# Normalisation and transposes of the next block between the K and V matmuls, and Q matmuls between the transposes of the query blocks

## What is computed

```python
def _layernorm(x, axis=-1, eps=1e-5):
    m = jnp.mean(x, axis=axis, keepdims=True)
    v = jnp.var(x, axis=axis, keepdims=True)
    return (x - m) / jnp.sqrt(v + eps)
...
        q = jnp.einsum('bsd,de->bse', X, Wq)
        k = jnp.einsum('bsd,de->bse', X, Wk)
        v = jnp.einsum('bsd,de->bse', X, Wv)
        scores = jnp.einsum('bqe,bke->bqk', q, k)
        causal = jnp.triu(jnp.ones((S, S), dtype=bool), k=1)
        scores = jnp.where(causal, -jnp.inf, scores)
        weights = jax.nn.softmax(scores / jnp.sqrt(jnp.asarray(k.shape[-1], scores.dtype)), axis=-1)
        return jnp.einsum('bqk,bke->bqe', weights, v)
...
        gate = jnp.einsum('bsd,hd->bsh', x, wg)
        up = jnp.einsum('bsd,hd->bsh', x, wu)
        h = jax.nn.silu(gate) * up
        return jnp.einsum('bsh,dh->bsd', h, wd)
...
    xn = _layernorm(x, axis=-1)
    s = _L0_attn_ref(xn, L0_attn_Wq, L0_attn_Wk, L0_attn_Wv)
    g = _silu(_L0_ffn_ref(xn, L0_ffn_w_gate, L0_ffn_w_up, L0_ffn_w_down))
    x = x + s * g
```

## Time and profile before

| | us |
|---|---|
| runs, lowest to highest | 2223.4 to 2234.1 |
| median of the 2 runs | 2228.7 |
| profiled execution | 2218.8 |
| its span, slowest core (core 4) | 2217.2 |
| span of the fastest core | 2193.0 |
| TensorE busy in matmuls | 1679.2 (76%) |
| ScalarE busy | 551.7 (25%) |
| VectorE busy | 535.1 (24%) |
| mean granted TensorE clock of the cores | 0.90 to 0.91 |

### The profile page before, as it was taken

The page is one execution under the profiler, slowest core; times in us unless marked ns, Lnnn a source line. Parts: engine busy times, 40 slices in busy tenths (PEclk is TensorE's granted clock), DMA queues, the critical chain, the costliest instruction groups (busy, mean ns, idle before and its releaser), DMA issues.

```text
span 2217.2 us, 24390 instructions; the slowest of 8 cores (2193.0 to 2217.2 us)
## 1 busy us (share of the span) xinstructions
PE 1679.2 (76%) x8391; PEld 804.1 (36%) x8544; DVE 535.1 (24%) x1356; ACT 551.7 (25%) x842; POOL 81.2 (4%) x149
## 2 busy tenths in 40 slices
PE   0333598898998964689989999875778787878875
PEld 0222344444444432334434444322333333333332
DVE  1000124334243344011100111003342233240430
ACT  0333433334333332211101111011222222221321
POOL 0000000000000000000000000000001000000000
PEclk9955599999999986889999999987999898989998
DMA  9998324344243341243310332037776775675934
GB/s 196 193 217 184 126 95 133 112 135 133 97 146 116 118 133 38 69 113 78 76 26 1 76 77 58 0 95 253 254 256 226 244 247 209 212 263 190 301 123 164
DMA packets 165751, 320.66 MB, mean 145 GB/s; under 512 B 105088, under 2 KB 111232, under 8 KB 143104
## 3 DMA queue, kind: packets, MB, share of 16 engines
q0 software_dynamic: 29968, 151.00, 23.9%
q1 hardware_dynamic: 124144, 149.20, 22.8%
q10 hardware_dynamic: 11520, 18.88, 2.4%
HBM read 283.41 MB, written 60.82 MB: 155 GB/s over the span
## 4 chain that ended last, share of the span: by engine, by line
PE 63%; DMA 17%; ACT 6%; another core or an unknown queue 4%; issue 4%; DVE 4%; ACTq 1%; SPq 1%; DVEq 0%; POOL 0%; POOLq 0%
PE psBC L404 11%; DMA vbuf<-vv_s 8%; PE psD L572 8%; PE psA L530 8%; PE psA L430 5%; PE psD L430 5%; PE psA L647 4%; PE psD L780 4%; PE psD L540 4%; PE psBC L540 4%; PE psBC L780 4%; DMA kbuf<-kT_s 3%; ACT xns L379 3%; PE psBC L473 3%
## 5 line engine op out<-in xcount | busy, mean ns | idle before, releaser
L404 PE MATMUL psBC<-xns,wk_b 128*128 128x512 bf16 x992 | 239.1, 403 | 27.9 <-ACT xns L379 27.1
L250 PE MATMUL psA<-ident_b,wst 128*128 128x128 bf16 x576 | 70.2, 297 | 188.9 <-DMA wst<-wg 86.3
L530 PE MATMUL psA<-xnq,wgu 128*128 128x512 bf16 x752 | 173.9, 381 | 29.1 <-DMA wgu<-wuT_s 28.3
L358 DVE TENSOR_SCALAR xnr<-xkb,mvall,rstdall 128x1024 bf16<-128x1024 f32 x80 | 61.8, 810 | 539.5 <-PE psA L370 537.2
L780 PE MATMUL psBC<-vbuf,pT 128*128 128x512 bf16 x494 | 133.8, 413 | 70.1 <-DMA vbuf<-vv_s 61.6
L572 PE MATMUL psD<-wdT_b,hact 128*128 128x512 bf16 x752 | 167.5, 379 | 22.1 <-ACT g_b L581 17.7
L404 PEld LDWEIGHTS psBC<-xns,wk_b 128*128 128x128 bf16 x1024 | 104.1, 103 | 157.9 <-issue 53.3
L647 PE MATMUL psA<-kbuf,qT 128*128 128x512 bf16 x598 | 138.0, 385 | 18.7 <-DMA kbuf<-kT_s 17.9
L780 PE MATMUL psD<-vbuf,pT 128*128 128x512 bf16 x562 | 141.3, 393 | 9.6 <-DMA vbuf<-vv_s 8.9
L755 ACT ACTIVATE pT<-psA 128x1024 bf16<-128x1024 bf16 x72 | 69.4, 976 | 262.5 <-PE psA L743 262.5
L250 PEld LDWEIGHTS psA<-ident_b,wst 128*128 128x128 bf16 x576 | 53.3, 133 | 205.6 <-issue 205.2
(11 more groups left out here) (83 smaller groups left out, 1634.1 us busy)
## 6 DMA issues: line engine op xcount, KB each, us to landing
vbuf<-vv_s POOLq DMA_DIRECT2D x72, 1024.0 KB, 5.6
kbuf<-kT_s SPq DMA_DIRECT2D x40, 1024.0 KB, 9.9
xkb<-xk SPq DMA_DIRECT2D x16, 2048.0 KB, 12.9
kbufX<-kT_s SPq DMA_DIRECT2D x32, 1024.0 KB, 13.3
kT_s<-kst POOLq DMA_DIRECT2D x16, 1024.0 KB, 4.3
vv_s<-vst POOLq DMA_DIRECT2D x16, 1024.0 KB, 6.8
wgu<-wgT_s SPq DMA_DIRECT2D x48, 256.0 KB, 3.2
wgu<-wuT_s SPq DMA_DIRECT2D x48, 256.0 KB, 4.6
```

The lines of the kernel that those rows point to most:

```text
L250: wfree=wfree, hpar=hpar: t.transpose(trA[:, par * 1024 + (rb - r0) * 128: par * 1024 + (rb - r0 + 1) * 128], wstf[:, hpar * 12288 + rb * ...
L404: (lambda t, dcc=dcc, pb=pb, e=e, ph=ph: t.matmul(psBC[:, ph * 512:(ph + 1) * 512], wk_b[:, dcc, e * 128:(e + 1) * 128], xns[:, pb, dcc, : ...
L530: gb=gb: t.matmul(psA[:, gb + sh * 512:gb + (sh + 1) * 512], wgu[:, par, 0, dcc, :], xnq[:, dcc, qs + sh * 512:qs + (sh + 1) * 512], start ...
```

## The change

`emit_norms` becomes `emit_ladder` and notes ScalarE's count behind its last copy in `xnsm[gb]`; `emit_kv` becomes `emit_K` and `emit_V`, and K waits for `xnsm[gb]` of its own block. The Q stage becomes `emit_Q(sb)`, one call for each query block, which waits for that block's `xnsm`. The loop now emits K(gb), the ladder of block gb+1, the load of gb+3, the statistics of gb+2, and V(gb). At the last K/V block, whose `xns` must be read before a query block is copied out, V comes ahead of the ladder. Behind it Q of a query block and the ladder of the next take turns. The barrier ahead of Q goes; two stand behind the loop.

```diff
-        def emit_norms(gb):
+        xnsm = {}
+
+        def emit_ladder(gb):
...
                 tr_evac.append(E.qsop("a", fn))
-
-        def emit_kv(gb):
+            xnsm[gb] = E.mark("a")
+
+        def emit_K(gb):
             src_h, lb, kv = entries[gb]
-            if not kv:
-                return
             pb = gb % 2
-            a_xns = E.mark("a")
+            a_xns = xnsm[gb]
...
+        def emit_V(gb):
+            src_h, lb, kv = entries[gb]
+            pb = gb % 2
...
-        for gb in range(NB):
-            emit_norms(gb)
-            if gb + 2 < NB:
-                emit_load(gb + 2)
-            if gb + 1 < NB:
-                emit_stats(gb + 1)
-            emit_kv(gb)
-
-    E.barrier()
-
-    if nphase >= 4:
-        q_evac = []
-        q_tmark = []
-        for sb in range(4):
+        def emit_Q(sb):
             for e in range(DC):
                 ph = e % 2
-                if len(q_evac) >= 2:
-                    E.qwait("t", "a", q_evac[-2])
-                q_tmark.append(E.qgroup("t", [
+                E.qwait("t", "a", xnsm[16 + sb])
+                if len(k_evac) >= 2:
+                    E.qwait("t", "a", k_evac[-2])
+                kv_tmark.append(E.qgroup("t", [
...
+        emit_stats(1)
+        emit_ladder(0)
+        emit_load(2)
+        for gb in range(NB):
+            kv = entries[gb][2]
+            boundary = kv and gb + 1 < NB and not entries[gb + 1][2]
+            if kv:
+                emit_K(gb)
+            elif nphase >= 4:
+                emit_Q(gb - 16)
+            if not boundary:
+                if gb + 1 < NB:
+                    emit_ladder(gb + 1)
+                if gb + 3 < NB:
+                    emit_load(gb + 3)
+                if gb + 2 < NB:
+                    emit_stats(gb + 2)
+            if kv:
+                emit_V(gb)
+            if boundary:
+                emit_ladder(gb + 1)
+                if gb + 3 < NB:
+                    emit_load(gb + 3)
+                if gb + 2 < NB:
+                    emit_stats(gb + 2)
+
+    E.barrier()
```

More of the change, by code:

```diff
@@ L478, in build @@
                     for dcc in range(DC)], "t"))
-                E.qwait("a", "t", q_tmark[-1])
-                q_evac.append(E.qsop("a", lambda a, sb=sb, e=e, ph=ph:
+                E.qwait("a", "t", kv_tmark[-1])
+                k_evac.append(E.qsop("a", lambda a, sb=sb, e=e, ph=ph:
                                      a.activation(
@@ L485, in build @@
                     func=AF.Copy)))
+        E.qwait("t", "a")
+        E.qwait("t", "wqkv")
+        emit_load(0)
+        emit_stats(0)
+        emit_load(1)
+        emit_stats(1)
[24 more added lines that the diff above has]
+    E.barrier()
     E.barrier()
```

## The result

The changed kernel took 2154.4 us in the median of 11 runs, beside 2224.5 for the kernel before (10 runs). The ratio is 0.967, interval 0.963 to 0.970; in a second set of runs it was 0.962 (0.959 to 0.966). Forecast were 2148 us against 2228.7 to 2223.4, a ratio of 0.964 to 0.966. The profiled execution took 2142.9 us, its span 2141.1 (core 7).

A forecast was written before the change was run, and what follows sets the result against it. TensorE's own order bounds the K/V stage, VectorE the query normalising, TensorE Q. Savings of 29 + 32 + 15 = 76 us from 2218.8 give 2142.8, plus 5 to reach the median: 2148 us, range 2127 to 2184.

The forecast's parts named there:

- 2. and 5.: Block 1's statistics ahead of the first ladder, covered, cost nothing; barrier behind the last Q stays in place, later stages only move forward.
- Step 1: K/V stage: next block's ladder between K and V, V starts 3.35 us behind its start; saves 29 us over 15 blocks.
- Step 4: K/V stage: shorter low stretch on TensorE gives back three quarters of 19.8 us of clock falls, 15 us.
- Step 3: Query blocks: ladder and Q in turn, 112.4 us becomes 80.4 with clock falls; saves 32 us.
- the margin of 2.5 us: Query stage: VectorE's statistics and remaining work finish 2.5 us before TensorE comes back for the next ladder.
- A: K/V stage: clock gives nothing back, as transposes themselves let it fall; 2163 us, 2185 with longest falls; chance 0.17.
- B: Query stage: VectorE or late loads set Q's pace, so all 32 us are lost; 2180 us; chance 0.06.
- D: K, V and Q: denser stage is granted less clock, at 0.8 costing 124 us, for 2282 us; chance 0.02.
- C: Attention stage stretches with another stagger of cores and gives back 42 us, for 2190 us; chance 0.07.

## Why the prediction was right

The time (2148 forecast, 2154.4 measured) and the sum agree, and so do terms 1 and 3; the clock was sized too low. Each is read from its own rows:

| term | forecast | measured |
|---|---|---|
| 1. ladder between K and V, 15 times | 29 | 29.3 (15 x (32.91 - 30.96)) |
| 4. clock in the K/V stage | 15 | 19.5 (19.8 before, less the 0.3 of the one longer period, which is a late copy) |
| 3. query stage | 32 | 30.7 (112.4 to 81.7) |
| 2. and 5. statistics, barrier | 0 | 1.2 (first ladder 263.63 to 262.42) + 1.6 (last Q copy to first gate matmul 28.2 to 26.6), unexplained |
| feed-forward and attention | 0 | -3.2 - 3.0, other core |
| sum | 76 | 76.1; the span shrank by 76.1 |

That the sum is right to a tenth is luck: 4.5 us more from the clock and 2.8 without an explanation stand against 1.3 less in the query stage and 6.2 in the later stages, which come from another core being the slowest.

*Step 1.* The model of the ladder, ScalarE's four copies behind one other copy, gave 3.35 us for TensorE and, with 27.62 of K and V, a period of 30.97; measured 3.33 and 30.96. The experiment with a V copy ahead gave 31.39 for 31.4 expected. So the part of the gain that looks least likely in a profile, 0.42 us from standing behind a shorter copy, is real: 6 of the 29 us.

*Step 4* was sized too low. The rows of before could not say what 3.35 us do, and three quarters was a choice; all of it came back, since no fall is left behind the 15 ladders. Experiments show that waiting inside the stretch brings the falls: with the order kept and V waiting 1.5 us longer the clock fell in every block, and with half a microsecond of wait in three to seven of 14. They lengthened the stretch by waiting alone, so its length and the idle time in it aren't told apart. They also show what the prediction did not say: falls aren't an even chance for each block. In the run with copy four awaited every block fell by the same 1.6 us, and the period held at 34.13. The longer stretch of the kernel before cost less in the mean (1.3). That the fall itself shifts the next ladder and so keeps the pattern going fits this, but wasn't isolated.

*Step 3.* All three interleaved ladders came at TensorE's pace, and VectorE was ready, as the margin of 2.5 us said. Each Q start fell, 1.4 to 1.7 us, 6.4 in all, beside 5 in the sum; the difference to 32 is that. With the ladders moved into Q, the falls and waits behind the three interleaved ladders went too; moving xns removed those of the first.

*The rivals.* A (the clock gives nothing back) is refuted by the rows; B (VectorE sets the pace of Q) by ladders 20.3 us apart with no wait for statistics; D by a granted clock of 0.99 in the denser stage. On a lower limit of the clock the Trainium skill ("TensorE: Matmul & The Clock Gate", Part 1) says to budget 1.95 GHz for sustained dense matmuls on all cores. The profiled executions of both kernels disagree, with a granted clock of 1.00 on all eight cores from 880 to 1398 us in the changed one; the profiled execution with a V copy ahead of the ladder's agrees, with 0.81 of 2.4 GHz on cores 0, 1, 6 and 7 in the K/V stage (periods of 37.44 us instead of 31.39) and on all eight from 1000 to 1400 us. So D's mechanism exists and shows in some executions; what sets it off was not tried.

*C, time coming back later,* was priced at 42 us from a share (5.7%) that no row gives. It asks for more than one core, since the slowest core was another one after the change (7 instead of 4). From the first gate matmul to the end of the span, core by core:

| core | 0 | 1 | 2 | 3 | 4 | 5 | 6 | 7 |
|---|---|---|---|---|---|---|---|---|
| before, start | 955.3 | 951.4 | 948.0 | 953.4 | 952.7 | 951.6 | 946.9 | 951.9 |
| before, rest | 1260.9 | 1249.7 | 1245.0 | 1263.5 | 1264.5 | 1264.3 | 1252.6 | 1249.8 |
| after, start | 871.6 | 876.6 | 876.3 | 871.3 | 871.5 | 876.1 | 874.8 | 870.4 |
| after, rest | 1241.4 | 1262.1 | 1258.0 | 1259.9 | 1255.5 | 1251.4 | 1263.8 | 1270.7 |

The start is that of the first gate matmul, the rest runs from there to the core's last instruction. The mean start moved from 951.4 to 873.6, 78 us; the mean rest from 1256.3 to 1257.9. So the later stages gave nothing back in the mean. They spread by 20 to 29 us over the cores, in another order each time, and the slowest core picks the largest: that is where the 6 us in the table and a part of the distance between executions of the same kernel come from. What makes the spread in attention was not tried.

## What to carry to other kernels

Of a short chain between engines (normalise, transpose, copy out) the steps in which the engine itself takes part stay (3.35 of 5.3 us here); the last steps cost time only where the next work of the waiting engine needs its result. Put the chain ahead of a piece of work that does not, however small: one V group of 3.45 us hid the copies as well as all four, and two of eight Q groups served the query blocks. And price the wait with the clock: a stretch of 5.3 us in which TensorE had only small transposes and waits made the next matmuls run at half clock for a while in 9 to 11 of 15 blocks, which here was worth two thirds as much again as the wait.

## What the runs showed that was not expected

The cost of falls does not grow steadily with the stretch. Per block it was 0 at 3.35 and at 3.76 us, 0.4 to 0.9 at 3.95, 1.6 at 4.9 (in every block, the same amount but for the first few) and 1.2 to 1.4 at 5.3 (9 to 11 of 15 blocks by core, 1.3 to 3.0 each). A wait of 0.45 us, which a view of core 4's waits sums to 6.8 us in the stage, brought falls worth 5 us (core 0) to 12 us (core 4); a profile of waits alone does not list them.

Also the pattern of falls is the same on all eight cores of the kernel before (periods of 34.4, 34.3, 34.2, 35.9, 32.9, 35.6, 32.9, 32.9 us, and then the same eight again; the cores stand at different places of it), though the cores don't wait for each other. That fits a pattern set by the block's length rather than by chance; no run isolated it.
